# Gated cross-attention layer: when the next head's keys and queries are loaded

## What is computed

```python
q = (x @ Wq + bq).reshape(1, B * N, H, hd)          # x is the layer norm of the input
kv = (cond @ Wkv + bkv).reshape(1, -1, 2, H, hd)
q = _fq_sym(q * scale, axis=-1)                      # rounded to 8-bit steps per row and head
k = _fq_sym(k, axis=-1)
v = _fq_sym(v, axis=2)
attn = softmax(einsum('bhqd,bhkd->bhqk', q, k))
attn = _fq_unsigned(attn, axis=-1)                   # rounded to 255 steps of the row's largest
out = einsum('bhqk,bhkd->bhqd', attn, v) @ Wp + bp
x = x + tanh(g_xattn) * out                          # then the feed-forward block in the same way
```

## Time and profile before

| | |
|---|---|
| median of three runs | 1850.08 us (1848.38 to 1850.37) |
| the profiled execution | 1850.08 us, with a span of 1848.3 us |
| VectorE busy | 1666.3 us (90%) |
| TensorE busy (matmul) | 1585.2 us (86%) |
| ScalarE busy | 1416.1 us (77%) |
| GpSimd busy | 1308.6 us (71%) |
| HBM and SBUF traffic of the DMAs | 269.80 MB, mean 146 GB/s |
| mean granted TensorE clock | 0.960 |

### The profile page before, as it was taken

One profiled execution on the slowest core, in us unless ns is written; L12 is line 12 of the kernel. 1 busy time (PEld: TensorE's weight loads), 2 busy tenths in 40 slices (PEclk: granted clock), 3 DMA queues, 4 the chain that ended last, 5 costly groups with the idle time before them and its releaser, 6 DMA issues. The chain is left out here.

```text
span 1848.3 us, 35492 instructions
## 1 busy us (share of the span) xinstructions
PE 1585.2 (86%) x13651; PEld 779.1 (42%) x13651; DVE 1666.3 (90%) x2239; ACT 1416.1 (77%) x1379; POOL 1308.6 (71%) x1293
## 2 busy tenths in 40 slices
PE   7799996898888888888888888888888886779995
PEld 4344441444444444444444444444444442323331
DVE  7778886999999999999999999999999993479894
ACT  4467777888888888888888887988888782677772
POOL 0144443898979988997999898899989896345530
PEclk9899996999999999999999999999999997889997
DMA  6746665999867889985799996678888874032313
GB/s 216 239 149 226 226 207 137 182 176 167 162 112 141 161 175 171 170 160 105 140 178 175 178 176 117 132 137 152 144 142 151 156 130 120 13 62 63 75 40 79
DMA packets 683721, 269.80 MB, mean 146 GB/s; under 512 B 610521, under 2 KB 641305, under 8 KB 682274
## 3 DMA queue, kind: packets, MB, share of 16 engines
q1 hardware_dynamic: 682178, 264.62, 68.4%
q0 software_dynamic: 704, 1.62, 0.2%
q10 hardware_dynamic: 672, 1.31, 0.2%
HBM read 84.20 MB, written 31.49 MB: 63 GB/s over the span
## 5 line engine op out<-in xcount | busy, mean ns | idle before, releaser
L911 DVE TENSOR_SCALAR_CACHE_REDUCE att_scaled<-att_scores,layer_nsq 128x1536 f32<-128x1536 f32 (+1 forms) x768 | 1200.2, 1632 | 14.4 <-PE att_scores L868 13.8
L931 POOL CAST att_probsT<-att_pairsT 128x2048 bf16<-128x2048 uint8 x512 | 953.6, 1891 | 93.2 <-DMA att_pairsT<-att_pairs 83.0
L982 ACT ACTIVATE att_pairs<-att_scaled,att_bias_row 128x4096 uint8<-128x4096 f32 x256 | 950.6, 3713 | 46.6 <-DMA att_pairsT<-att_pairs 28.8
L868 PE MATMUL att_scores<-first_k_head,first_q_head 96*128 96x512 bf16 x1024 | 299.3, 397 | 90.6 <-DVE att_scaled L911 75.6
L868 PE MATMUL att_scores<-att_k_head,att_q_head 96*128 96x512 bf16 x1024 | 285.8, 381 | 63.9 <-DVE att_scaled L911 60.9
L882 PEld LDWEIGHTS att_ps_o<-att_v_head,att_probsT 128*128 128x128 bf16 x8192 | 242.8, 96 | 71.7 <-POOL att_probsT L931 10.3
L882 PE MATMUL att_ps_o<-att_v_head,att_probsT 128*128 128x32 bf16 x8192 | 245.2, 177 | 7.8 <-ACT layer_o_sum L974 4.3
L868 PEld LDWEIGHTS att_scores<-first_k_head,first_q_head 96*128 96x128 bf16 x1024 | 81.9, 99 | 252.2 <-DVE att_scaled L911 171.3
L846 PE MATMUL att_scores<-att_k_head,att_q_head 96*128 96x512 bf16 x651 | 175.9, 379 | 0.0
L846 PE MATMUL att_scores<-first_k_head,first_q_head 96*128 96x512 bf16 x600 | 168.9, 393 | 0.0
L868 PEld LDWEIGHTS att_scores<-att_k_head,att_q_head 96*128 96x128 bf16 x1024 | 79.2, 97 | 209.3 <-DVE att_scaled L911 149.9
(11 more groups left out here) (163 smaller groups left out, 1729.2 us busy)
## 6 DMA issues: line engine op xcount, KB each, us to landing
layer_w2T<-ctx_T SPq DMA_DIRECT2D x96, 256.0 KB, 3.8
k_parts<-kv_k_stage SPq DMA_DIRECT2D x16, 768.0 KB, 5.1
q_w_in<-in_L_ffn_w_dram SPq DMA_DIRECT2D x32, 256.0 KB, 2.9
kv_weights_ctx_in<-in_ctx_dram SPq DMA_DIRECT2D x32, 256.0 KB, 5.1
kv_weights_w_in<-in_L_ffn_w_dram SPq DMA_DIRECT2D x32, 256.0 KB, 5.0
ctx_T<-kv_inT SPq DMA_DIRECT2D x8, 1024.0 KB, 6.1
att_k_head<-k_parts SPq DMA_DIRECT2D x96, 64.0 KB, 3.0
first_k_head<-k_parts SPq DMA_DIRECT2D x84, 64.0 KB, 2.8
```

Of the source, the lines that this page charges most:

```text
L868: last = pe.matmul(buffer[:, x:x + 512], q_head[slot][:, at:at + P], k_head[slot][:, STARTS[j] + x:STARTS[j] + x + 512], start=True, stop= ...
L911: dve.tensor_scalar(scaled[u][:, STARTS[j]:STARTS[j] + WIDTHS[j]], scores[(g * NCH + j) % 2][:, 0:WIDTHS[j]], kept["nsq"][:, g:g + 1], Non ...
L931: pool.tensor_copy(probsT[g % C_BUFS][:, parity * HALF:(parity + 1) * HALF, :].rearrange("p k q -> p (k q)"), turned.rearrange("p (n two) ...
L982: act.activation(pairs[g % R_BUFS][:, :].bitcast(U8).rearrange("p (c two) -> p two c", two=2), scaled[u][:, :].rearrange("p (two c) -> p t ...
```

## The change

Two lines of `attend` are altered. Before, the pieces of the next head go out in units 1 to 12 of a head, one piece of keys in each unit, with a piece of queries added in units 1, 3 and 5. Afterwards they go out in units 5 to 12: one piece of keys in units 5, 7, 9 and 11, two in units 6, 8, 10 and 12, and a piece of queries in units 5, 7 and 9. The number and size of the transfers are the same. Before the first piece SyncE's queue waited until all scores of head h-2 were computed; now it waits until the products with the values of all units of head h-2 are computed.

```diff
-        LOAD_UNITS, PER_PART, FIRST_PIECE = 12, 4, 1
+        LOAD_UNITS, PER_PART, FIRST_PIECE = 8, 4, 5
...
                     h, i = g // QT + 1, g % QT - FIRST_PIECE
                     if 0 <= i < LOAD_UNITS and h < H:
                         if i == 0:
-                            after(sp, scores_ready, (h - 1) * QT * NCH)
+                            after(sp, pv_ready, (h - 1) * QT)
                         load_piece(h, i)
```

## The result

The changed kernel takes 1859.47 us, the median of seven runs (1856.22 to 1868.67), against 1850.08 us. The ratio of the paired runs is 1.0065, with a 95% interval of 1.0045 to 1.0086: 12.0 us slower (8.3 to 15.9) on 1850. The direction was forecast; the size was not (5.4 us were).

A forecast was written before the change was run, and what follows sets the result against it. VectorE was taken to bound the attention stage, idling where keys land late at heads 2, 6 and 10. Terms 3.0 + 2.2 + 0.7 - 0.5 = 5.4 us on 1850.1 gave 1855.5 us, range 1852 to 1860.

The forecast's parts named there:

- parts 2 and 3: SyncE's queue: paired last keys 0.48 us later, added pieces another 0.48; 1.0 us at heads 2, 6, 10, sum 3.0.
- Part 1: SyncE's queue at unit 5: the new wait is met over 13 us early, so it costs 0.
- part 6: Starts of heads other than 2, 6 and 10: last piece lands in time, 0 to 0.3 us for all, taken as 0.
- parts 2 to 5: Starts of heads 2, 6 and 10: queue delay 3.0 us, DMA overload 2.2 us and clock 0.7 us.
- part 4: DMA engines in units 5 to 12: 512 KB moved in, 4.4 us doesn't fit; half taken, 2.2 us.
- Its own sign against it: DMA share in units 5 to 12: if it doesn't rise, the DMA overload term is undone.
- Part 5: TensorE's clock at head 10's start: a wait of 2.2 us should lower it too, costing 0.7 us.
- Part 7: Units 1 to 4, free of 512 KB: transposes land sooner, ScalarE is less behind at unit 5; gain 0.5 us.
- faster: Rival: GpSimd and ScalarE catch up by unit 5, the last piece leaves earlier; ceiling 6.0 us, 1846 us; chance 0.08.
- no-change rival: SyncE's queue: pieces may only shorten slow transposes, leaving 1.4 us for the pair; 1850 to 1852 us; chance 0.30.
- much slower one: Rival: whole DMA overload, and heads 1, 5 and 9 begin to wait; 13.2 us, 1863 us; chance 0.10.

The follow-up runs named there:

- again: The changed kernel run once more with no edit, for a second trace: 1860.49 us, ratio 1.0076 to the kernel before.
- oldwait: The changed kernel with the old wait (scores of head h-2) in place of the new one: 1862.48 us, ratio 1.0081 to the kernel before.
- early8: The changed kernel with the same bunching in units 1 to 8 and the old wait: 1846.39 us, ratio 0.9988 to the kernel before.
- units4to11: The changed kernel one unit earlier, pieces in units 4 to 11, pair and new wait kept: 1849.94 us, ratio 1.0006 to the kernel before.
- even_last: The changed kernel with keys two by two in units 5 to 8 and single in 9 to 12: 1862.13 us, ratio 1.0072 to the kernel before.
- queries_early: The changed kernel with its pieces of queries back in units 1, 3 and 5, behind the old wait: 1855.41 us, ratio 1.0040 to the kernel before.
- tiny_issues: The changed kernel with queries back in units 1, 3 and 5, old wait, and 2 KB DMAs in units 7 and 9: 1856.92 us, ratio 1.0048.
- turn13: The changed kernel with the transpose of the next head's values in unit 13 in place of 9: 1850.12 us, ratio 1.0015 to the kernel before.
- units0to11: The kernel before with its pieces, one to a unit, in units 0 to 11 in place of 1 to 12: 1844.49 us, ratio 0.9976.
- units0to11_turn13: The kernel before with pieces in units 0 to 11 and the transpose of the values in unit 13, not 9: 1856.76 us, ratio 1.0032.

## Why the forecast was right and where it was wrong

The bound and the mechanism were right. The last piece of keys for a head was late already, it became later, and VectorE idles for it (parts 2 and 3; again, oldwait, early8, units4to11). Part 1, the new wait at no cost, was right (oldwait).

The size was wrong, and the step that failed most is part 6, the other starts. "Their last piece lands in time" was true before, and the prediction set them at 0 to 0.3 us. Measured from VectorE's idle rows, they cost 2.6 us in again (heads 5, 9, 13, 14 and 15) and 7.0 us in oldwait (heads 5, 9, 13 and 14). The room there had been 0.5 to 1.7 us, and the last piece came later by more than that. Head 15 is indeed the tightest, but it was given a second piece (0.58 us) and no delay of the queue, and the other five were not priced. With heads 2, 6 and 10 the starts cost 9.8 us more than before in again and 12.6 us more in oldwait, of 10.1 and 12.7 us by which the attention stage grew. That accounts for the measured loss of 12.0 us.

At heads 2, 6 and 10 the sum was about right, and in part by luck. Forecast were 5.9 us with parts 2 to 5, about 2 us each. Measured in again: 5.34 - 2.37 = 3.0, 3.51 - 3.10 = 0.4 and 4.42 - 0.53 = 3.9 us, sum 7.3. In oldwait: 2.9, -0.6 and 3.3 us, sum 5.6. Head 6, to which part 4 gave the most, lost next to nothing. Of the terms:

- Parts 2 and 3 had the last piece for head 2 come 1.0 us later. It came 2.5 us later: the pair went out 1.4 us late, its second piece 0.5 behind, and landing took 3.9 us in place of 3.4. The delay was priced from unit 9 on, at 0.48 us by unit 10. The queue was 1.4 us behind by the transpose of unit 9 already, and 2.1 by unit 10. even_last and queries_early show that what units 5 to 8 hold counts too.
- Part 4 took half of the overfilled DMA time. The 4.4 us whole would have given 7.6. Its own sign against it came out in one place of three: ahead of head 10 the DMA share fell, 0.95 to 0.92, where the wait grew much. So the share is a poor witness, and tiny_issues leaves open how much of the price is bytes and how much is issue time. The price itself, 3.3 us for 512 KB, is weak as well. By the queue's rows, 10 pieces of keys and 2 of queries are issued in the first of its two windows and not 11 and 3, and that window also holds a transpose of the values, which the second lacks.
- Part 5, the clock, came true at head 10, which now pays with 0.49 us and first scores of 1.46 us, at a clock of 0.83. Its yardstick, the length of the wait, doesn't hold: after waits of 2.03 and 3.15 us in oldwait the clock stayed at 1.00 (last section).
- Part 7, the relief of units 1 to 4, was booked as a gain of 0.5 us. No run shows one. ScalarE's exponential of unit 5 in heads 1, 5 and 9 starts behind VectorE's first part of that unit by 7.2 us on average before, 8.4 in again and 7.3 in oldwait, worked out from the timelines; nothing was caught up by unit 5. The rival that rested on it, faster, is refuted by the time.

The no-change rival is refuted by the interval. The much slower one, given a chance of 0.10, comes nearest with its 13.2 us. It had two halves: starts of heads 1, 5 and 9 that begin to wait, and the overload of part 4 taken whole. The first is where the missing size is: TensorE waits at all three, and VectorE idles at heads 5 and 9, and at 13 to 15 as well. Its sign, VectorE waiting for ScalarE in the middle of a head, was not seen beyond one wait of 0.7 us.

## What to carry to other kernels

A prefetch that "ends four units early" in the issuing loop may end with no slack in time: compare the landing of its last piece with the first use, per round, before thinning it out at the front. When a queue is nearly full, price a moved transfer at the sum over the whole crowded stretch, not at the one slot in which it lands; one instruction out of that stretch (turn13) or one slot of distance (units4to11) gave most of the loss back. A delay that is added at every round has to be set against the room of every round, not only of those that wait already. The fastest version tried here is the simplest: the kernel before, started one unit earlier, 0.9976 (0.9965 to 0.9986).

## What the runs showed of the hardware

- How long a DMA transpose holds SyncE's queue varies widely: the same transpose of the values, ahead of head 2, took 1.64 us before, 1.27 in again and 3.14 in even_last. Counting issues at their shortest price understates a full queue.
- Two kernels that differ in the place of one instruction per head spread very differently over twelve executions each: units0to11 by 6 us (1839.96 to 1846.14), units0to11_turn13 by 21 us (1840.85 to 1861.54). Why isn't shown. One profiled execution, even a typical-looking one, can miss the difference that is sought.
- TensorE's granted clock after a wait for keys doesn't follow from the length of the wait. In the 10 us from the first scores it was 1.00, the higher level (2.4 GHz) throughout, after waits of 1.20 us (before, head 10), 1.72 (again, head 5), 2.03 and 3.15 us (oldwait, heads 9 and 6). It was lower, part of the window at the lower level (1.2 GHz), after 1.76 and 3.17 us (before, heads 2 and 6: 0.83 both), 2.56 and 2.82 us (oldwait, heads 5 and 10: 0.71 and 0.68), 3.97 and 4.60 us (again, heads 10 and 2: 0.84 and 0.81).
